# One masked conditional matrix kernel: where the first masks are loaded, and which engine masks and splits around units 5 to 7

## The chip, the core and the metric

One NeuronCore of a Trainium2 chip. The metric is the device time of one execution in microseconds, the median over several runs. Engines by name: TensorE (PE; weight loads are listed apart as PEld), VectorE (DVE), ScalarE (ACT), GpSimd (POOL) and SyncE (SP), which issues most DMAs.

## The reference

```
masked_w = weight * mask[None, :, :]            # weight (8, 256, 256), mask (256, 256)
w_bot    = einsum('bg,got->bot', y, masked_w)   # y (32, 8)
out      = x + einsum('bnt,bot->bno', x, w_bot) + bias   # x (32, 256, 256), fp32
```

For each of 32 batch entries a 256x256 matrix is mixed from 8 masked weight matrices; x is multiplied by it (and by the identity, for the residual), and a bias is added.

## The kernel before

**Making the matrices.** The 32 matrices live transposed in `w_raw` (t on partitions, o on columns). They are made in 8 units of 32 output rows (`UNITS`, `SPAN`), two units to a pair. The rows of a unit fall into a diagonal side, on which the identity must be added, and another ("off") side. The weights of the diagonal side are multiplied by the mask ahead of the matmuls ("masked" loads: 512 columns of weights and 512 of mask side by side, into a staging place in `x_ring`; the product goes into `blocks`), and PE starts these banks with a 0/1 matmul that writes the identity (L326). The weights of the other side go in unmasked ("other" loads), and the mask is applied when the PSUM result is copied into `w_raw`: by VectorE (L635) for all units but unit 1, where ScalarE copies (L516) and GpSimd masks in place (L315, four instructions, semaphore `raw_masked`). ScalarE copies the diagonal side of each unit (L534; VectorE L631 for unit 1). PE's small matmuls are `weigh` (L332).

Who masks the diagonal weights: VectorE pairs 0 and 3 (L581, two halves each, `masked_by_dve`), GpSimd pairs 1 and 2 (L306, `masked_by_pool`).

**The products.** x comes in 8 groups of 4 batch entries. Group 0 is multiplied in plain fp32 (L451): 8 matmuls ("early", between units 5 and 6; ScalarE evicts them at L531) and 24 more after unit 7. Groups 1 to 7 are multiplied as three matmuls of rounded numbers each: high weights by high x (L431), high weights by low x (L432), low weights by high x (L433). ScalarE casts the high parts (L491 x, L499 and L502 weights), VectorE subtracts the low ones (L589 x, L598 and L605 weights). Group 1's weights are split in three pieces (`pieces`): half of the batch entries of output half 0, the other half of them, and all of output half 1. Group 2 is split whole.

**Order.** Each engine's order is written out by hand. SP issues: other 0, masked 0, masked 1, other 1, off (masks of the off sides of units 2 to 7), masked 2, other 2, half of x group 0, masked 3, other 3, the other half, group 1; then, waiting for the masks of pairs 0 and 1, group 2, and for those of pairs 2 and 3, group 3. ScalarE's queue loads `smalls` (y, bias, the off masks of units 0 and 1) first. ScalarE around unit 6: copy of unit 5, pieces 0 and 1 (L502), early eviction (L531), copies of units 6 and 7, then, once all of `w_raw` is there, piece 2, high x of group 1 in two halves, high weights and x of group 2. VectorE there: units 4, 5 (L635), masks of pair 3 (L581), low pieces 0 and 1 (L605), units 6 and 7, then low piece 2, low x of group 1, and so on. PE's batch of 24 starts when seven copies of ScalarE are done (`raw_by_act`, `UNITS - 1`, L471), and its last 16 when all copies are (L474, L475). PE's unit 2 needs other 1 and, for its diagonal side, masks of pair 1 by GpSimd.

## Time and profile before

| | us |
|---|---|
| median of 3 runs | 66.35 (66.0 to 66.44) |
| span of the profiled execution | 65.5 |
| PE busy / DVE / ACT / POOL | 58.8 / 48.1 / 47.9 / 7.0 |
| PE's granted clock | 0.999 of 2.4 GHz |

The span runs from the first to the last instruction of one profiled execution; the median is of timed runs, which hold what lies around the span too. A row of a timeline gives start, duration, engine, line, operation, output and inputs, count, and in brackets the idle time before it and what ended it. Rows of like instructions that follow each other are merged, and their duration then runs from the first start to the last end.

### The profile page before, as it was taken

To read this page: it belongs to the slowest core of one execution; us is meant where nothing else is said; L and a number is where in the kernel's file an instruction comes from. 1 tells how busy PE (TensorE), PEld (TensorE's weight loads), DVE (VectorE), ACT (ScalarE), POOL (GpSimd) and SP (SyncE) were. 2 spreads that over 40 slices of the span, in tenths; PEclk is the share of its full clock that TensorE was granted. 3 is DMA by queue.
4 is the path that set the end of the run, shared out by engine and by line. 5 is a ranking of instruction groups with operands and counts; after the bars stand their busy time and mean duration, and the time that the engine had idled before them with its cause. 6 is when DMAs were issued, how large, how long until landed. Compare 5 with 4: busy or idle time off the path is not lost.

```text
span 65.5 us, 1501 instructions
## 1 busy us (share of the span) xinstructions
PE 58.8 (90%) x645; PEld 54.3 (83%) x645; DVE 48.1 (73%) x36; ACT 47.9 (73%) x40; POOL 7.0 (11%) x17
## 2 busy tenths in 40 slices
PE   2997188999999999999999999999999999999910
PEld 1266087977888899999999999999999999999900
DVE  2109809999957989999999999989999992250200
ACT  2506609799889999999999799999869986005520
POOL 5500299900000000000000000000000000000000
PEclk9999999999999999999999999999999999999999
DMA  0999999999998157954999999999999229918393
GB/s 0 260 373 306 352 412 422 407 434 428 420 410 340 60 85 255 408 215 198 245 285 225 400 451 420 403 441 423 398 413 425 93 100 408 398 63 325 158 372 116
DMA packets 5334, 20.21 MB, mean 309 GB/s; under 512 B 592, under 2 KB 1104, under 8 KB 4432
## 3 DMA queue, kind: packets, MB, share of 16 engines
q1 hardware_dynamic: 5040, 19.89, 79.6%
q10 hardware_dynamic: 288, 0.23, 1.1%
q8 instruction: 5, 0.08, 0.5%
q14 instruction: 1, 0.01, 0.1%
HBM read 11.73 MB, written 8.39 MB: 307 GB/s over the span
## 4 chain that ended last, share of the span: by engine, by line
PE 79%; DMA 9%; ACT 4%; SPq 2%; issue 1%
PE slots L433 20%; PE slots L431 20%; PE slots L432 20%; PE slots L451 11%; DMA weights<-in_first 9%; PE slots L332 6%; ACT w_raw L534 3%; PE slots L326 2%; ACT weights L563 1%; SPq L230 1%; SPq L222 1%; SPq L229 1%
## 5 line engine op out<-in xcount | busy, mean ns | idle before, releaser
L431 PE MATMUL slots<-x_hi,w_hi 128*128 128x256 f32 x112 | 31.4, 280 | 0.0
L432 PE MATMUL slots<-x_lo,w_hi 128*128 128x256 f32 x112 | 31.2, 279 | 0.0
L433 PE MATMUL slots<-x_hi,w_lo 128*128 128x256 f32 x112 | 31.2, 279 | 0.0
L431 PEld LDWEIGHTS slots<-x_hi,w_hi 128*128 128x128 f32 x112 | 21.1, 188 | 0.0
L432 PEld LDWEIGHTS slots<-x_lo,w_hi 128*128 128x128 f32 x112 | 21.1, 188 | 0.0
L433 PEld LDWEIGHTS slots<-x_hi,w_lo 128*128 128x128 f32 x112 | 21.1, 188 | 0.0
L589 DVE TENSOR_TENSOR x_lo<-x_ring,x_hi 128x2048 fp32r<-128x2048 f32 (+1 forms) x8 | 16.1, 2022 | 0.5 <-ACT x_hi L491 0.5
L491 ACT CAST x_hi<-x_ring 128x2048 fp32r<-128x2048 f32 (+1 forms) x8 | 13.5, 1694 | 1.3 <-DMA x_ring<-in_x 1.3
L511 ACT ACTIVATE weights<-slots,smalls 128x1024 f32<-128x1024 f32 x10 | 10.8, 1112 | 4.7 <-PE slots L433 4.7
L598 DVE TENSOR_TENSOR w_lo<-w_raw,w_hi 128x2048 fp32r<-128x2048 f32 x6 | 13.7, 2288 | 0.2 <-ACT w_hi L499 0.2
L499 ACT CAST w_hi<-w_raw 128x2048 fp32r<-128x2048 f32 x6 | 11.5, 1909 | 0.0
L332 PE MATMUL slots<-smalls,weights 32*128 32x128 f32 x256 | 9.3, 279 | 2.0 <-DMA weights<-in_first 1.6
L332 PEld LDWEIGHTS slots<-smalls,weights 32*128 32x128 f32 x256 | 8.2, 186 | 3.0 <-DVE w_raw L631 1.9
L534 ACT COPY w_raw<-slots 128x1024 f32<-128x1024 f32 x7 | 7.0, 1014 | 3.8 <-PE slots L332 3.7
L635 DVE TENSOR_TENSOR w_raw<-slots,masks_off 128x1024 f32<-128x1024 f32 x6 | 7.1, 1220 | 2.0 <-PE slots L332 1.8
L451 PE MATMUL slots<-x_ring,w_raw 128*128 128x256 f32 x32 | 7.4, 386 | 0.2
L451 PEld LDWEIGHTS slots<-x_ring,w_raw 128*128 128x128 f32 x32 | 5.9, 190 | 1.3 <-ACT w_raw L534 0.5
L615 DVE TENSOR_SCALAR weights<-slots,smalls 128x1024 f32<-128x1024 f32 x4 | 5.1, 1282 | 2.4 <-PE slots L433 2.4
L581 DVE TENSOR_TENSOR weights<-x_ring 128x256 f32<-128x256 f32 x4 | 1.5, 420 | 3.1 <-DMA x_ring<-in_first 3.1
L306 POOL TENSOR_TENSOR weights<-x_ring 128x256 f32<-128x256 f32 x4 | 2.8, 727 | 5.2 <-ACT w_raw L534 5.0
L440 PE MATMUL slots<-zeros 128*128 128x512 bf16 x5 | 2.3, 626 | 1.2 <-DVE zeros L571 1.2
L605 DVE TENSOR_TENSOR w_lo<-w_raw,w_hi 128x512 fp32r<-128x512 f32 (+1 forms) x3 | 2.5, 866 | 1.2 <-ACT w_hi L502 1.2
(25 smaller groups left out, 19.3 us busy)
## 6 DMA issues: line engine op xcount, KB each, us to landing
out<-weights SPq DMA_DIRECT2D x15, 512.0 KB, 4.7
x_ring<-in_x SPq DMA_DIRECT2D x7, 1024.0 KB, 9.6
x_ring<-in_first SPq DMA_DIRECT2D x6, 512.0 KB, 7.2
weights<-in_first SPq DMA_DIRECT2D x4, 256.0 KB, 6.6
out<-weights SPq DMA_DIRECT2D x1, 256.0 KB, 2.4
out<-weights SPq DMA_DIRECT2D x1, 128.0 KB, 2.3
out<-weights ACTq DMA_DIRECT2D x1, 128.0 KB, 2.1
smalls<-in_small ACTq DMA_DIRECT2D x1, 97.0 KB, 3.1
```

The source lines that it names most:

```text
L332: return nc.tensor.matmul(bank(u, i)[:, q * B * RT:(q + 1) * B * RT], weights_of(u, i // PER)[rows, q * P:(q + 1) * P], y[rows], start=not ...
L431: nc.tensor.matmul(dst, wh, xh, start=(k == 0), stop=False)
L432: nc.tensor.matmul(dst, wh, xl, start=False, stop=False)
L433: last = nc.tensor.matmul(dst, wl, xh, start=False, stop=(k == KC - 1))
L451: last = nc.tensor.matmul(dst[:, (b - lo) * N:(b - lo + 1) * N], w_raw[:, b, k * O + h * P:k * O + (h + 1) * P], x_ring[:, 0, first_x(k, b ...
L491: nc.scalar.copy(part_x(x_hi[:, g % RS], lo, hi), part_x(x_ring[:, g % XS], lo, hi)).then_inc(x_hi_ready, 1)
L499: nc.scalar.copy(part(w_hi, g), raw_part(g)).then_inc(w_hi_ready, 1)
L511: nc.scalar.activation(result(g, h), product(g, h), ACT.Identity, bias=bias(h)).then_inc(done, 1)
L534: nc.scalar.copy(raw_slot(u, True), made(u, True)).then_inc(raw_by_act, 1)
L589: nc.vector.tensor_tensor(part_x(x_lo[:, g % RS], lo, hi), part_x(x_ring[:, g % XS], lo, hi), part_x(x_hi[:, g % RS], lo, hi).bitcast(F32) ...
L598: nc.vector.tensor_tensor(part(w_lo, g), raw_part(g), part(w_hi, g).bitcast(F32), ALU.subtract).then_inc(w_lo_ready, 1)
L635: nc.vector.tensor_tensor(raw_slot(u, False), made(u, False), mask_off_of(u).unsqueeze(2).broadcast_to([P, PER * QU, B, RT]), ALU.mult).th ...
```

## The change

The masks of pair 0 depend on the output row and t, not on the group, so each stands 8 times in the 128 partitions. They are now loaded once, a quarter per partition (`mask_in`, 128 columns, at the end of `smalls`), and VectorE spreads them with four stream shuffles into the place where the loaded masks stood. VectorE masks half 0 of pair 0, GpSimd half 1 (`first_by_pool`). The off masks of units 0 and 1 leave `smalls` for a DMA of their own on ScalarE's queue (`first_offs`), and the bias goes to the end of the "off" load. GpSimd also masks pair 3, and makes pieces 0 and 1 of group 1's low weights (`w_lo_by_pool`). ScalarE casts output half 0 of group 2's weights ahead of the early eviction, the pieces 0 and 1 behind it, and piece 2 behind high x of group 1; VectorE subtracts that half of group 2 between units 5 and 6. PE gets one more matmul of zeros (512 columns) in unit 2. The two functions `lows_of` and `highs_of` give the semaphore counts that follow.

```diff
--- before.py
+++ after.py
@@ -43,21 +43,24 @@
 ORDER = (("other", 0), ("masked", 0), ("masked", 1), ("other", 1), ("off", 0), ("masked", 2), ("other", 2), ("x", 0),
          ("masked", 3), ("other", 3), ("x", 1))
-COLUMNS = {"masked": SLOT, "other": BANK, "off": (UNITS - SIDES) * SPAN, "x": WIDE // 2}
-AT_BIAS = B * RT
-AT_MASKS = AT_BIAS + HO
-SMALL = AT_MASKS + SIDES * SPAN
-def conditional_residual(nc, x, small, first, out):
+FIRST = {("masked", 0): BANK}
+COLUMNS = {"masked": SLOT, "other": BANK, "off": (UNITS - SIDES) * SPAN + HO, "x": WIDE // 2}
+CHUNKS = 4
+CHUNK = BANK // CHUNKS
+AT_SPREAD = B * RT
+SMALL = AT_SPREAD + CHUNK
+AT_BIAS = (UNITS - SIDES) * SPAN
+def conditional_residual(nc, x, small, first_off, first, out):
     assert QU * P == BANK and SLOT == 2 * BANK and O == N == T and QU * B * RT == BANK
-    assert SPAN * TILES == P and QU * RT * 2 == ROWS and KC == HO == SIDES == PER == 2 and TILES == QU == NB == SLOTS == PAIRS
+    assert SPAN * TILES == P and QU * RT * 2 == ROWS and KC == HO == SIDES == PER == 2 and TILES == QU == NB == SLOTS == PAIRS and CHUNKS <= G
     with ExitStack() as ctx:
         def sb(name, shape, dt=F32):
@@ -77,7 +80,8 @@
         weights = sb("weights", [P, SLOTS, SLOT])
-        masks_off = sb("masks_off", [P, UNITS - SIDES, PER * QU, RT])
+        offs = sb("offs", [P, COLUMNS["off"]])
+        first_offs = sb("first_offs", [P, SIDES, SPAN])
         smalls = sb("smalls", [P, SMALL])
         x_ring = sb("x_ring", [P, XS, WIDE])
         x_hi = sb("x_hi", [P, RS, WIDE], F32R)
@@ -104,22 +108,22 @@
             return blocks[:, 2 * (u // 2) + (side != diagonal_side(u)), :]
         def in_order(what, j):
-            at = P * sum(COLUMNS[kind] for kind, i in ORDER[:ORDER.index((what, j))])
-            return first[at:at + P * COLUMNS[what]].rearrange("(p f) -> p f", p=P)
+            at = P * sum(FIRST.get((kind, i), COLUMNS[kind]) for kind, i in ORDER[:ORDER.index((what, j))])
+            return first[at:at + P * FIRST.get((what, j), COLUMNS[what])].rearrange("(p f) -> p f", p=P)
         y = smalls[:, 0:B * RT]
         def mask_off_of(u):
             if u < SIDES:
-                return smalls[:, AT_MASKS + u * SPAN:AT_MASKS + (u + 1) * SPAN].rearrange("p (m r) -> p m r", r=RT)
-            return masks_off[:, u - SIDES]
+                return first_offs[:, u].rearrange("p (m r) -> p m r", r=RT)
+            return offs[:, (u - SIDES) * SPAN:(u - SIDES + 1) * SPAN].rearrange("p (m r) -> p m r", r=RT)
         def half_of(i):
             return slice(i * BANK // 2, (i + 1) * BANK // 2)
         def bias(h):
-            return smalls[:, AT_BIAS + h:AT_BIAS + h + 1]
+            return offs[:, AT_BIAS + h:AT_BIAS + h + 1]
         smalls_loaded = sem("smalls_loaded")
         zeroed = sem("zeroed")
@@ -129,7 +133,10 @@
         one_zeroed = sem("one_zeroed")
         one_ready = sem("one_ready")
-        masks_off_loaded = sem("masks_off_loaded")
+        mask_spread = sem("mask_spread")
+        first_by_pool = sem("first_by_pool")
+        first_offs_loaded = sem("first_offs_loaded")
+        offs_loaded = sem("offs_loaded")
         masked_loaded = [sem(f"masked_loaded{j}") for j in range(PAIRS)]
         others_loaded = [sem(f"others_loaded{j}") for j in range(PAIRS)]
         masked_by_dve = sem("masked_by_dve")
@@ -149,6 +156,7 @@
         x_lo_ready = sem("x_lo_ready")
         w_hi_ready = sem("w_hi_ready")
         w_lo_ready = sem("w_lo_ready")
+        w_lo_by_pool = sem("w_lo_by_pool")
         early_ready = sem("early_ready")
         early_by_act = sem("early_by_act")
         products_ready = sem("products_ready")
@@ -176,6 +184,14 @@
         pieces = ((0, NB // 2, 0), (NB // 2, NB, 0), (0, NB, 1))
+        def lows_of(g, h):
+            return g + 1 if g > 2 else (None, (None, 2), (1, 3))[g][h]
+        def highs_of(g, h):
+            return g + 3 if g > 2 else (None, (3, 4), (1, 5))[g][h]
         def raw_part(g, lo=0, hi=NB, h=None):
             v = w_raw[:, NB * g + lo:NB * g + hi, :]
             return v if h is None else v.rearrange("p b (k o) -> p b k o", k=KC)[:, :, :, h * P:(h + 1) * P]
@@ -227,9 +243,9 @@
                 return sp.dma_start(x_ring[:, 0, i * SLOT:(i + 1) * SLOT], in_order("x", i))
             sp.dma_start(blocks[:, 1, :], in_order("other", 0)).then_inc(others_loaded[0], 16)
-            sp.dma_start(staged(0), in_order("masked", 0)).then_inc(masked_loaded[0], 16)
+            sp.dma_start(staged(0)[:, 0:BANK], in_order("masked", 0)).then_inc(masked_loaded[0], 16)
             load_pair(1)
-            sp.dma_start(masks_off[:].rearrange("p u m r -> p (u m r)"), in_order("off", 0)).then_inc(masks_off_loaded, 16)
+            sp.dma_start(offs[:], in_order("off", 0)).then_inc(offs_loaded, 16)
             load_pair(2)
             load_half(0).then_inc(half_x_loaded, 16)
             load_pair(3)
@@ -237,12 +253,12 @@
             load_group(1)
-            sp.wait_ge(masked_by_dve, 2)
+            sp.wait_ge(masked_by_dve, 1)
+            sp.wait_ge(first_by_pool, 1)
             sp.wait_ge(masked_by_pool, 2)
             load_group(XS - 2)
-            sp.wait_ge(masked_by_pool, 2 * (PAIRS - 2))
-            sp.wait_ge(masked_by_dve, 4)
+            sp.wait_ge(masked_by_pool, 2 * (PAIRS - 1))
             load_group(XS - 1)
             for g in range(GROUPS - 1):
@@ -298,8 +314,13 @@
                 one_of[:], firsts[:, 0:QU * RT].rearrange("p (q r) -> p q r", r=RT).unsqueeze(2).broadcast_to([P, QU, B, RT]),
             ).then_inc(one_ready, 1)
-            behind_pair = (None, (0,), (1, 2, 3))
-            for j in range(1, PAIRS - 1):
+            pool.wait_ge(masked_loaded[0], 16)
+            pool.wait_ge(mask_spread, CHUNKS)
+            nc.gpsimd.tensor_tensor(blocks[:, 0, half_of(1)], staged(0)[:, 0:BANK][:, half_of(1)],
+                                    staged(0)[:, BANK:SLOT][:, half_of(1)], ALU.mult).then_inc(first_by_pool, 1)
+            behind_pair = (None, (0,), (1, 2, 3), ())
+            for j in range(1, PAIRS):
                 pool.wait_ge(masked_loaded[j], 16)
                 for i in range(2):
@@ -308,12 +329,18 @@
                 if j == 1:
-                    pool.wait_ge(smalls_loaded, 16)
+                    pool.wait_ge(first_offs_loaded, 16)
                     pool.wait_ge(raw_by_act, 1)
                 for i in behind_pair[j]:
                     some = raw_columns(1, False)[:, i * MB:(i + 1) * MB, :]
-                    nc.gpsimd.tensor_tensor(some, some, smalls[:, AT_MASKS + SPAN:AT_MASKS + 2 * SPAN].unsqueeze(1).broadcast_to(
+                    nc.gpsimd.tensor_tensor(some, some, first_offs[:, 1].unsqueeze(1).broadcast_to(
                         [P, MB, SPAN]), ALU.mult).then_inc(raw_masked, 1)
+            for i in range(HO):
+                pool.wait_ge(w_hi_ready, i + 2)
+                nc.gpsimd.tensor_tensor(part(w_lo, 1, *pieces[i]), raw_part(1, *pieces[i]), part(w_hi, 1, *pieces[i]).bitcast(F32),
+                                        ALU.subtract).then_inc(w_lo_by_pool, 1)
         @block.tensor
         def _(pe):
@@ -350,9 +377,12 @@
                         if q == QU - 1:
                             last.then_inc(others_ready, 1)
                 for q in range(QU):
-                    if q % 2 == 0:
-                        pe.wait_ge(masked_by_dve, q // 2 + 1)
+                    if q == 0:
+                        pe.wait_ge(masked_by_dve, 1)
+                    if q == QU // 2:
+                        pe.wait_ge(first_by_pool, 1)
                     for u in range(SIDES):
                         for i in range(PER):
                             last = weigh(u, on[u] + i, q)
@@ -374,6 +404,8 @@
                     pe.wait_ge(early_by_act, 1)
                 identity(u, on)
                 identity(u, on + 1)
+                if u == SIDES:
+                    nc.tensor.matmul(bank(u, on), zeros[:, 0:P], zeros[:], start=False, stop=False)
                 pe.wait_ge(raw_by_dve, u - 1)
                 if u % 2 == 0:
@@ -382,10 +414,7 @@
                 weigh(u, off, 0)
                 weigh(u, off + 1, 0)
                 for q in range(QU):
-                    if u == EARLY and q % 2 == 0:
-                        pe.wait_ge(masked_by_dve, 3 + q // 2)
-                    elif u % 2 == 0 and q % 2 == 0:
+                    if u % 2 == 0 and q % 2 == 0:
                         pe.wait_ge(masked_by_pool, u - 1 + q // 2)
                     weigh(u, on, q)
@@ -401,7 +430,10 @@
                 pe.wait_ge(x_lo_ready, 1 if g == 1 else g + 1)
-                pe.wait_ge(w_lo_ready, 1 if g == 1 else g + len(pieces) - 1)
+                if g == 1:
+                    pe.wait_ge(w_lo_by_pool, 1)
+                else:
+                    pe.wait_ge(w_lo_ready, lows_of(g, 0))
                 for h in range(HO):
                     if g >= 2 and h == 0:
@@ -417,10 +449,10 @@
                         if g == 1 and h == 0 and b == NB // 2:
                             pe.wait_ge(x_lo_ready, 2)
-                            pe.wait_ge(w_lo_ready, 2)
-                        if g == 1 and h == 1 and b == 0:
-                            pe.wait_ge(w_lo_ready, len(pieces))
+                            pe.wait_ge(w_lo_by_pool, 2)
+                        if g <= 2 and h == 1 and b == 0:
+                            pe.wait_ge(w_lo_ready, lows_of(g, 1))
                         if g == GROUPS - 1 and h == 1 and b == NB - 1:
                             pe.wait_ge(out0_by_act, g)
@@ -481,6 +513,7 @@
         @block.scalar
         def _(act):
             act.dma_start(smalls[:], small).then_inc(smalls_loaded, 16)
+            act.dma_start(first_offs[:].rearrange("p u f -> p (u f)"), first_off).then_inc(first_offs_loaded, 16)
             def high_x(g, lo=0, hi=NB):
@@ -490,13 +523,13 @@
                     act.wait_ge(products_ready, HO * (g - RS + 1))
                 nc.scalar.copy(part_x(x_hi[:, g % RS], lo, hi), part_x(x_ring[:, g % XS], lo, hi)).then_inc(x_hi_ready, 1)
-            def high_weights(g):
+            def high_weights(g, h=None):
                 act.wait_ge(raw_masked, NB * g // MB + 1)
                 if g > RS:
                     act.wait_ge(products_ready, HO * (g - RS + 1))
-                nc.scalar.copy(part(w_hi, g), raw_part(g)).then_inc(w_hi_ready, 1)
+                nc.scalar.copy(part(w_hi, g, 0, NB, h), raw_part(g, 0, NB, h)).then_inc(w_hi_ready, 1)
             def high_piece(i):
                 nc.scalar.copy(part(w_hi, 1, *pieces[i]), raw_part(1, *pieces[i])).then_inc(w_hi_ready, 1)
@@ -522,24 +555,24 @@
                     act.wait_ge(raw_by_act, UNITS // HO)
                     act.wait_ge(raw_by_dve, UNITS // HO)
-                    act.wait_ge(raw_masked, 1)
+                    high_weights(2, 0)
+                    act.wait_ge(offs_loaded, 16)
+                    act.wait_ge(early_ready, 1)
+                    nc.scalar.activation(result(0, 0)[:, 0:BANK], early, ACT.Identity, bias=bias(0)).then_inc(early_by_act, 1)
                     high_piece(0)
                     high_piece(1)
-                    act.wait_ge(smalls_loaded, 16)
-                    act.wait_ge(early_ready, 1)
-                    nc.scalar.activation(result(0, 0)[:, 0:BANK], early, ACT.Identity, bias=bias(0)).then_inc(early_by_act, 1)
                 act.wait_ge(diagonal_ready, u + 1)
                 nc.scalar.copy(raw_slot(u, True), made(u, True)).then_inc(raw_by_act, 1)
             act.wait_ge(raw_by_act, UNITS)
             act.wait_ge(raw_by_dve, UNITS)
-            high_piece(2)
             for lo in (0, NB // 2):
                 high_x(1, lo, lo + NB // 2)
-            high_weights(2)
+            high_piece(2)
             high_x(2)
+            high_weights(2, 1)
             act.wait_ge(products_ready, 1)
             nc.scalar.activation(result(0, 0)[:, BANK:SLOT], product(0, 0)[:, BANK:SLOT], ACT.Identity,
@@ -574,14 +607,19 @@
             nc.vector.tensor_reduce(firsts[:], ident[:].rearrange("p (i f) -> p f i", i=TILES), axis=AX_X,
                                     op=ALU.add).then_inc(firsts_ready, 1)
-            def mask_pair(j):
+            def mask_pair(j, halves):
                 dve.wait_ge(masked_loaded[j], 16)
-                for i in range(2):
+                for i in halves:
                     nc.vector.tensor_tensor(blocks[:, 2 * j, half_of(i)], staged(j)[:, 0:BANK][:, half_of(i)],
                                             staged(j)[:, BANK:SLOT][:, half_of(i)], ALU.mult).then_inc(masked_by_dve, 1)
-            mask_pair(0)
+            dve.wait_ge(smalls_loaded, 16)
+            for c in range(CHUNKS):
+                nc.vector.stream_shuffle(staged(0)[:, BANK + c * CHUNK:BANK + (c + 1) * CHUNK], smalls[:, AT_SPREAD:AT_SPREAD + CHUNK],
+                                         [G * (r // G) + c for r in range(ROWS)]).then_inc(mask_spread, 1)
+            dve.wait_ge(mask_spread, CHUNKS // 2)
+            mask_pair(0, (0,))
             def low_x(g, lo=0, hi=NB):
@@ -589,20 +627,13 @@
                 nc.vector.tensor_tensor(part_x(x_lo[:, g % RS], lo, hi), part_x(x_ring[:, g % XS], lo, hi),
                                         part_x(x_hi[:, g % RS], lo, hi).bitcast(F32), ALU.subtract).then_inc(x_lo_ready, 1)
-            def low_weights(g):
-                dve.wait_ge(w_hi_ready, g + len(pieces) - 1)
+            def low_weights(g, h=None):
+                dve.wait_ge(w_hi_ready, highs_of(g, h))
                 if g > LS:
                     dve.wait_ge(products_ready, HO * (g - LS + 1))
-                nc.vector.tensor_tensor(part(w_lo, g), raw_part(g), part(w_hi, g).bitcast(F32),
-                                        ALU.subtract).then_inc(w_lo_ready, 1)
-            def low_piece(i):
-                dve.wait_ge(w_hi_ready, i + 1)
-                nc.vector.tensor_tensor(part(w_lo, 1, *pieces[i]), raw_part(1, *pieces[i]), part(w_hi, 1, *pieces[i]).bitcast(F32),
+                nc.vector.tensor_tensor(part(w_lo, g, 0, NB, h), raw_part(g, 0, NB, h), part(w_hi, g, 0, NB, h).bitcast(F32),
                                         ALU.subtract).then_inc(w_lo_ready, 1)
             def finish(g):
@@ -615,15 +646,13 @@
                 nc.vector.tensor_scalar(result(g, 1), product(g, 1), bias(1), None,
                                         ALU.add).then_inc(out1_by_dve, 1)
-            dve.wait_ge(smalls_loaded, 16)
+            dve.wait_ge(first_offs_loaded, 16)
             for u in range(UNITS):
                 if u == SIDES:
-                    dve.wait_ge(masks_off_loaded, 16)
+                    dve.wait_ge(offs_loaded, 16)
                 if u == EARLY:
-                    mask_pair(PAIRS - 1)
-                    low_piece(0)
-                    low_piece(1)
+                    low_weights(2, 0)
                 if u == 1:
@@ -636,11 +665,11 @@
                                         mask_off_of(u).unsqueeze(2).broadcast_to([P, PER * QU, B, RT]),
                                         ALU.mult).then_inc(raw_by_dve, 1)
-            low_piece(2)
             for lo in (0, NB // 2):
                 low_x(1, lo, lo + NB // 2)
-            low_weights(2)
+            low_weights(1, 1)
             low_x(2)
+            low_weights(2, 1)
             finish(0)
             for g in range(1, GROUPS - 1):
                 if g + 2 < GROUPS:
...
+    mask_in = np.stack([diagonal[1][p, p % G % CHUNKS * CHUNK:(p % G % CHUNKS + 1) * CHUNK] for p in range(P)])
+    loads["masked", 0] = diagonal[0]
...
+    loads["off", 0] = np.concatenate([other_off, bias.reshape(HO, P).T], axis=1)
...
+    small = np.concatenate([y.reshape(P, B * RT), mask_in], axis=1)
```

## Rows read from the trace of the kernel before

**Rows 1.** The page: its head, and the chain's shares by engine and by line.
```profile
span 65.5 us, 1501 instructions
...
PE 79%; DMA 9%; ACT 4%; SPq 2%; issue 1%
PE slots L433 20%; PE slots L431 20%; PE slots L432 20%; PE slots L451 11%; DMA weights<-in_first 9%; PE slots L332 6%; ACT w_raw L534 3%; PE slots L326 2%; ACT weights L563 1%; SPq L230 1%; SPq L222 1%; SPq L229 1%
```

**Rows 2.** The chain that ended last, in order of time: start us, us, what.
```profile
2.11 6.18 DMA weights<-in_first
...
8.43 1.34 PE slots L332 x30
...
13.42 1.99 PE slots L451 x8
...
16.68 1.02 ACT w_raw L534
17.75 5.45 PE slots L451 x24
```

**Rows 3.** Busy us by stretches, 30 to 40: PE, PEld, DVE, ACT, POOL, clock, DMA.
```profile
30.00:40.00 10.00, 10.00 (x88) 10.00 (x87) 10.00 (x6) 9.63 (x7) 0.00 (x0) 1.00 0.94 324
```

**Rows 4.** Transfers: a stretch (GB/s last), the queues, two issues, two landings.
```profile
2.50:8.50 6.00, 4.00 (x77) 2.29 (x75) 3.03 (x4) 2.02 (x2) 0.95 (x3) 1.00 0.99 356
...
q1 hardware_dynamic: 5040, 19.89, 79.6%
q10 hardware_dynamic: 288, 0.23, 1.1%
...
0.75 0.40 ACTq L483 DMA_DIRECT2D smalls<-in_small  x1
...
5.09 0.66 SPq L222 DMA_DIRECT2D x_ring<-in_first  x1
...
smalls<-in_small ACTq DMA_DIRECT2D x1, 97.0 KB, 3.1
...
x_ring<-in_first SPq DMA_DIRECT2D x1, 512.0 KB, 9.1
```

**Rows 5.** Timeline of ACT, 14 to 22 us.
```profile
14.39 1.14 ACT L502 CAST w_hi<-w_raw 128x512 fp32r<-128x512 f32 x2
15.52 0.69 ACT L531 ACTIVATE weights<-slots,smalls 128x512 f32<-128x512 f32 x1
16.68 2.00 ACT L534 COPY w_raw<-slots 128x1024 f32<-128x1024 f32 x2 [0.48 <-PE slots L332]
19.01 1.05 ACT L502 CAST w_hi<-w_raw 128x1024 fp32r<-128x1024 f32 x1 [0.33 <-DVE w_raw L635]
19.96 2.00 ACT L491 CAST x_hi<-x_ring 128x1024 fp32r<-128x1024 f32 x2
```

**Rows 6.** Timeline of DVE, 1 to 34 us.
```profile
1.50 0.37 DVE L574 TENSOR_REDUCE firsts<-ident 128x32 f32<-128x128 f32 x1 [0.37 <-POOL ident L284]
4.99 0.76 DVE L581 TENSOR_TENSOR weights<-x_ring 128x256 f32<-128x256 f32 x2 [3.11 <-DMA x_ring<-in_first]
...
14.57 0.75 DVE L581 TENSOR_TENSOR weights<-x_ring 128x256 f32<-128x256 f32 x2
...
16.56 2.36 DVE L635 TENSOR_TENSOR w_raw<-slots,masks_off 128x1024 f32<-128x1024 f32 x2
20.09 1.23 DVE L605 TENSOR_TENSOR w_lo<-w_raw,w_hi 128x1024 fp32r<-128x1024 f32 x1 [1.17 <-ACT w_hi L502]
...
31.60 2.29 DVE L598 TENSOR_TENSOR w_lo<-w_raw,w_hi 128x2048 fp32r<-128x2048 f32 x1
```

**Rows 7.** Timeline of POOL, 7 to 14 us.
```profile
7.71 1.41 POOL L306 TENSOR_TENSOR weights<-x_ring 128x256 f32<-128x256 f32 x2 [5.05 <-ACT w_raw L534]
...
9.91 1.42 POOL L306 TENSOR_TENSOR weights<-x_ring 128x256 f32<-128x256 f32 x2 [0.20 <-DMA x_ring<-in_first]
11.29 1.84 POOL L315 TENSOR_TENSOR w_raw<-w_raw,smalls 128x256 f32<-128x256 f32 x3
```

10 lines of the change are left out of this document (5 added, 5 removed).

## The prediction

> **What bounds the kernel now.** I read first the page's head and its chain that ended last [rows 1]: 65.5 us of span, 79% of the chain on PE. Then the chain piece by piece, in order of time [rows 2]. It falls into two parts. From 17.75 us on it is PE alone: 24 matmuls of line 451 take 5.45 us, to 23.20, and group 1 follows without a pause. Groups 1 to 7 (L431, L432, L433, each 20% of the span on the chain, [rows 1]) are 39.3 us, 5.6 a group, to about 62.5; in the stretch from 30 to 40 us PE is busy 10.00 of 10.00 [rows 3]. The last eviction and store end the span. The diff leaves this part alone. So the time falls only if the batch that starts at 17.75 starts earlier.
>
> What sets 17.75? Read [rows 2] backwards: ACT's copy of unit 6 (L534, 16.68 to 17.70; L471 counts seven copies, that one among them), before it the early product (L451 x8, 13.42 to 15.41) and units 6 and 7, before that units 2 to 5, in which PE and ACT take turns, and before 8.43 a wait for pair 1's unmasked rows, which landed at 2.11 + 6.18 = 8.29. A transfer, then a chain of some 9.3 us.
>
> **How far the transfers move.** "masked 0" falls from 512 to 256 KB. The smalls grow from 97 KB (194 columns) to 128 KB (256 columns), and 32 KB (64 columns) become a DMA of their own, with 256 bytes per partition. In all 193 KB fewer lie ahead of masked 1 and other 1; "off" gains 8 bytes per partition, nothing. From 2.5 to 8.5 us the queues moved 356 GB/s [rows 4], at which 262 thousand bytes are 0.74 us; by queue q1's mean (79.6% of 16 engines x 65.5 us for 19.89 MB, so 42 ns per thousand bytes of one engine) they are 0.69. Against it stand 31 KB more of smalls, 0.09 us, and the new DMA: by its bytes 0.09 us, by its 128 packets at q10's mean (288 packets in 1.1% of 16 x 65.5 us, 40 ns each) 128 x 40 / 16 ns = 0.32 us. So the loads behind land earlier by S = 0.74 - 0.09 - 0.09 = 0.56 us by the kind prices and 0.69 - 0.09 - 0.32 = 0.28 by the dear ones. I take 0.45, a little above the middle, for this reason: GpSimd could start on masked 1 at 7.71 [rows 7], VectorE on masked 0 at 4.99 [rows 6]: 2.7 us for 512 KB, which are 1.5 us at 356 GB/s, so some of the 16 engines ran behind the mean. If removed bytes count at the pace of the laggards (1672 thousand bytes landed between about 2.0 and 8.3 us, 265 GB/s), S is 198 / 265 = 0.75. That is the upper end.
>
> All that follows 8.43 moves by S, for units 2 to 5 wait for one another and for loads that move alike (masked 2, for which GpSimd waited 0.20 us until 9.91, [rows 7]).
>
> **The first pair.** The smalls were issued at 0.75 and landed 3.1 later, at 3.85 [rows 4], and will at 3.95. VectorE then spreads them with four shuffles of 128 columns. No row has one. From below: VectorE's subtraction takes 1.23 us for 1024 columns and 2.29 for 2048, 1.04 ns a column, and the two 256-column masks 0.76 together, so some 0.36 each; 128 columns fewer make 0.23. From above: the reduction of 128 columns, 0.37 [rows 6]. Four of them are 0.9 to 1.5 us. I take 0.25 each, since a copy stands nearer to the mask than a reduction does, and the spread ends at 4.95. Half 0 is masked at 5.35 (at dearest 5.9) instead of 5.4. GpSimd's half takes 0.73 [rows 7] and is there at 5.7 to 6.2, or at 6.6 if it must wait for VectorE's; PE comes to it some 0.6 us after it starts. The pair's weighs (1.3 us for as many, [rows 2]) end at 6.6 to 7.3. The cover is the wait for other 1, now until 8.29 - 0.45 = 7.84: this costs nothing. Without that cover it would be up to 0.7 us. The zero matmul added at unit 2 (512 columns; it can't be dearer than the 0.6 that remain, being one instruction among matmuls of 0.28) lies in the same wait. ScalarE's second DMA issue (the first is 0.40 us, [rows 4]) comes before its table load, long before its first copy.
>
> The Trainium skill (VectorE: DVE Perf Modes, The perf-mode tier table) gives a stream shuffle about 2400 ns for 2048 elements whatever the type; an estimate by it, 0.15 us of streaming each and a fixed part, would lie near my lower bound. No row of before shows one.
>
> **The middle, units 5 to 7.** Here work moves between engines, and the sum turns on ScalarE [rows 5]. Before: from 14.39 the two pieces (1.14 together; start to start a row is 0.10 shorter, as 19.01 + 1.05 against 19.96 shows), at 15.52 the early eviction behind its product (15.41), then 0.48 us idle, and at 16.68 unit 6's copy. After, in the old times less S: the cast of the third group's first half (128x1024, as the row at 19.01, 0.95 start to start) takes the place at 14.39 and is through at 15.34; the early eviction still starts with its product, at 15.52; 0.59 later, at 16.11, the two pieces, 1.04; unit 6's copy at 17.15. PE's unit 6 is done by 16.65, so the copy now waits for ScalarE itself. 17.15 against 16.68: of 0.95 us added, 0.48 fill the idle time and **0.47 go onto the path**. PE's batch of 24 then starts at 17.75 + 0.47 - S = 17.77 with S = 0.45.
>
> VectorE [rows 6] loses the masks of pair 3 and pieces 0 and 1 (14.57 to 16.56) and gains half of the third group's low (128x1024, 1.23). It can start when the cast ends, 15.44 - 0.45 = 15.0, to 16.2; units 6 and 7 (2.36) follow to 18.6, before 18.92. PE needs unit 7's result (L475) 8 matmuls into the batch, at 17.8 + 1.8 = 19.6: no gain, no loss. GpSimd: masked 3 landed at 5.09 + 9.1 = 14.19 [rows 4] and now at 13.75; GpSimd is free by 13.13 - 0.45; the two halves (1.41, [rows 7]) end at 15.2. PE starts unit 6 at 14.9 and asks for the second half some 0.7 us later: hidden, with 0.4 to spare. Then it makes pieces 0 and 1 of the low matrices, 512 columns each. No row has that form on GpSimd; by its masks (0.69 per 256 columns, start to start) one is 1.4 us, and if the rounding form is twice as dear, 2.8. From 16.7 on they end at 19.5 or 22.3. Group 1 needs them at 23.2: nothing. SP's load of x for group 3 waits for the masks of pair 3, at 15.2 against 14.57 + 0.75 = 15.3: nothing.
>
> **What is late next.** If PE did start earlier, would it run into VectorE? The low matrices of group 3 are ready at 31.60 + 2.29 = 33.89 [rows 6], needed at 23.2 + 2 x 5.6 = 34.4: 0.5 us to spare. The change makes this 1.7, since a half of 1.2 us moves ahead of the batch. So no later wait eats a gain; but there is none to eat.
>
> **The sum**, against the profiled 65.5 us: -0.45 (transfers) + 0.47 (ScalarE) = 0.0. The runs shown have a median of 66.35, 0.85 above this span; the same distance is to be added after. I forecast 66.3, as S has more room above my value than below.
>
> **The rivals.**
> *A. Removed bytes count at the laggards' pace*: S = 0.75, gain 0.28, 66.05. For it speaks the 2.7 us between masked 0 and masked 1; against it that the mean rate of all engines doesn't show it.
> *B. The shift comes through whole*, ScalarE's cast being hidden: gain 0.45 to 0.75, 65.9 to 65.6. Against it: ScalarE's order is written out, and 0.48 us is all its idle time there.
> *C. The small packets and the shuffles eat the shift*: S at 0.28 or lower, to 0; or shuffles of 0.6 us each, by which the first pair ends near 8.0. Loss 0.2 to 0.47, 66.55 to 66.8.
> *D, the other side: VectorE and GpSimd shut each other out.* If VectorE's low half (15.0 to 16.2, both inputs in SBUF) starts before GpSimd's second half of pair 3 (due at 14.45), and the later has to wait for the earlier, GpSimd ends at 16.9, PE's unit 6 near 17.6, its copy at 18.65, and the batch starts at 18.7: 0.95 us late, 67.3. It decides from the point where masked 3 lands more than 0.55 us later than 13.75. GpSimd's two pairs of masks took 1.41 and 1.42 us, with VectorE idle for much of the first and at work for the second [rows 6, 7], but at work on matrices in PSUM, so the trace doesn't refute it. In the forecast's order the same would cost VectorE 0.2 us, of which it has 1.0.
> The Trainium skill (SBUF — State Buffer, Who interferes with whom) says that a VectorE instruction with two SBUF inputs and a GpSimd instruction that reads SBUF block one another for a whole instruction. By that rule the shutting out is real and only the order decides whether the time is 66.3 or 67.3.
>
> **How the numbers follow.** Forecast (66.15 to 66.5) 0.50; A 0.18; B 0.10; C 0.14; D 0.08. The range, 65.85 to 66.8, holds the forecast, A and C and leaves out D and most of B. A measurement of this kernel tells some 1%, 0.66 us, from no change. Faster by more: B with a large S, and a little beyond A, 0.12. Slower by more: D, and what lies beyond C, 0.12. Within it 0.76.
>
> **What would show it.** After: PE's first weigh of unit 2 at 7.9 to 8.1; no idle time on ScalarE before unit 6's copy, at about 16.7; line 451's batch at 17.7 to 17.8, group 1 right behind it at 23.2. The forecast is wrong if the batch starts before 17.4 (then ScalarE's cast was hidden, or S is large), or after 18.0 with PE waiting inside unit 6 (then D).

## The result, and the profile after

| | before | after |
|---|---|---|
| median, us | 66.33 (6 runs) | 67.15 (6 runs) |
| span, median of the timed runs' own spans | 64.6 (113 later runs, 64.2 to 65.9) | 64.95 (6 runs, 64.6 to 65.5) |
| time less span, median | 1.80 (1.74 to 1.90) | 2.19 (2.17 to 2.23) |
| span of the profiled execution | 65.5 | 64.9 |

The changed kernel is slower by 1.3%: ratio 1.013, 95% interval 1.0098 to 1.0162. I had forecast 66.3. Ratios, and from here on the medians of span and of time less span, leave out executions over 1.5% above the fastest of their kernel; times, and the spans of the kernel before in this table, leave out none. Yet its profile shows a shorter span than the one before, 64.9 against 65.5. Both are true, and the table says how. Every timed run also gives its span. The kernel before has spans from 64.2 to 65.9 in 113 runs with a median of 64.6 (64.5 by the rule for ratios), and 108 of them are shorter than the 65.5 of the profile that I read; and the time is 1.80 us more than the span, not the 0.85 that I got by taking the median of other runs less that one span. After, the time is 2.19 more than the span. So the loss of 0.8 us is 0.35 to 0.45 in the span and 0.4 outside it.

The page of the kernel after, its head and the chain's shares by engine (compare [rows 1]):

```profile
span 64.9 us, 1516 instructions
...
PE 77%; ACT 8%; DMA 6%; issue 2%; DVE 2%; ACTq 0%
```

Its chain in order of time (start us, us, what), against [rows 2]:

```profile
0.74 3.69 DMA smalls<-in_small
...
4.46 0.67 DVE x_ring L619 x5
...
5.27 0.42 DVE weights L614
...
5.74 1.31 PE slots L359 x32
7.05 0.20 PE slots L353 x2
7.26 0.32 PE slots L408
7.58 1.17 PE slots L359 x32
...
13.37 1.05 ACT w_hi L532
...
14.49 0.69 ACT weights L562
15.18 1.02 ACT w_hi L535 x2
16.20 0.92 ACT w_raw L567
...
17.17 5.45 PE slots L483 x24
```

Two things have changed. The transfer that stood on the chain (other 1) is gone from it: in its place stands the load of the smalls, then the shuffles, half 0's mask and the pair's weighs, then the new matmul of zeros, and unit 2 starts at 7.58. And from 13.37 to 17.12 the chain is ScalarE without a break: cast, early eviction, two pieces, copy of unit 6.

ScalarE's timeline of the same stretch, against [rows 5]:

```profile
13.37 1.05 ACT L532 CAST w_hi<-w_raw 128x1024 fp32r<-128x1024 f32 x1
14.49 0.69 ACT L562 ACTIVATE weights<-slots,offs 128x512 f32<-128x512 f32 x1
15.08 1.13 ACT L535 CAST w_hi<-w_raw 128x512 fp32r<-128x512 f32 x2
16.11 1.93 ACT L567 COPY w_raw<-slots 128x1024 f32<-128x1024 f32 x2
```

The 0.48 us of idle time before unit 6's copy is gone. From the first cast to that copy it is 16.11 - 13.37 = 2.74 us; before it was 16.68 - 14.39 = 2.29. That is 0.45 more.

### The profile page after: what moved, and what is told of

It reads as the page before. It is cut to its first block, busy times and chain, and to the rows that moved or that the text cites. A ratio compares the mean times of both kernels' runs of the same rounds, so it can differ in the third digit from the quotient of the medians.

```text
span 64.9 us, 1516 instructions
## 1 busy us (share of the span) xinstructions
PE 59.5 (92%) x646; PEld 54.4 (84%) x646; DVE 47.4 (73%) x40; ACT 47.9 (74%) x41; POOL 12.1 (19%) x22
## 4 chain that ended last, share of the span: by engine, by line
PE 77%; ACT 8%; DMA 6%; issue 2%; DVE 2%; ACTq 0%
PE slots L464 20%; PE slots L463 20%; PE slots L465 20%; PE slots L483 8%; PE slots L359 7%; DMA smalls<-in_small 6%; ACT w_raw L567 3%; ACT w_hi L532 2%; ACT w_hi L535 2%; PE slots L353 1%; ACT weights L562 1%; DVE x_ring L619 1%; ACT weights L596 1%; DVE weights L614 1%; PE slots L408 0%
## 5 line engine op out<-in xcount | busy, mean ns | idle before, releaser
L463 PE MATMUL slots<-x_hi,w_hi 128*128 128x256 f32 x112 | 31.4, 280 | 0.0
L463 PEld LDWEIGHTS slots<-x_hi,w_hi 128*128 128x128 f32 x112 | 21.1, 188 | 0.0
L636 DVE TENSOR_TENSOR w_lo<-w_raw,w_hi 128x2048 fp32r<-128x2048 f32 (+1 forms) x8 | 15.5, 1931 | 0.8 <-ACT w_hi L532 0.8
L544 ACT ACTIVATE weights<-slots,offs 128x1024 f32<-128x1024 f32 x10 | 10.8, 1111 | 5.1 <-PE slots L465 5.1
L532 ACT CAST w_hi<-w_raw 128x2048 fp32r<-128x2048 f32 (+1 forms) x7 | 11.6, 1662 | 0.0
L567 ACT COPY w_raw<-slots 128x1024 f32<-128x1024 f32 x7 | 7.0, 1015 | 1.7 <-PE slots L359 1.5
L664 DVE TENSOR_TENSOR w_raw<-slots,offs 128x1024 f32<-128x1024 f32 x6 | 7.1, 1216 | 0.5 <-PE slots L359 0.4
L646 DVE TENSOR_SCALAR weights<-slots,offs 128x1024 f32<-128x1024 f32 x4 | 5.1, 1280 | 2.4 <-PE slots L465 2.4
L327 POOL TENSOR_TENSOR weights<-x_ring 128x256 f32<-128x256 f32 x6 | 4.3, 730 | 1.7 <-DMA x_ring<-in_first 1.5
L684 DVE TENSOR_SCALAR weights<-slots,offs 128x256 f32<-128x256 f32 x1 | 0.5, 483 | 3.6 <-PE slots L465 3.6
L549 ACT COPY w_raw<-slots 128x1024 f32<-128x1024 f32 x1 | 1.0, 1012 | 2.8 <-PE slots L359 2.8
```

The lines of the kernel that those rows point to most:

```text
L463: nc.tensor.matmul(dst, wh, xh, start=(k == 0), stop=False)
L532: nc.scalar.copy(part(w_hi, g, 0, NB, h), raw_part(g, 0, NB, h)).then_inc(w_hi_ready, 1)
L544: nc.scalar.activation(result(g, h), product(g, h), ACT.Identity, bias=bias(h)).then_inc(done, 1)
L567: nc.scalar.copy(raw_slot(u, True), made(u, True)).then_inc(raw_by_act, 1)
L636: nc.vector.tensor_tensor(part(w_lo, g, 0, NB, h), raw_part(g, 0, NB, h), part(w_hi, g, 0, NB, h).bitcast(F32), ALU.subtract).then_inc(w_l ...
L664: nc.vector.tensor_tensor(raw_slot(u, False), made(u, False), mask_off_of(u).unsqueeze(2).broadcast_to([P, PER * QU, B, RT]), ALU.mult).th ...
```

## The experiments

All times are medians of runs timed beside runs of the kernel before on the same chip; "time less span" is taken run by run. Two questions: where the 0.4 us outside the span come from, and where the gain of the transfers went.

**1. A fourth input tensor?** The off masks moved behind the smalls in one DRAM tensor:

```diff
-            act.dma_start(smalls[:], small).then_inc(smalls_loaded, 16)
-            act.dma_start(first_offs[:]..., first_off).then_inc(first_offs_loaded, 16)
+            act.dma_start(smalls[:], small[0:P * SMALL].rearrange("(p f) -> p f", p=P)).then_inc(smalls_loaded, 16)
+            act.dma_start(first_offs[:]..., small[P * SMALL:].rearrange("(p f) -> p f", p=P)).then_inc(first_offs_loaded, 16)
```

> The changed kernel, with one difference: the off masks of units 0 and 1 lie behind the smalls in the same DRAM tensor, so the program has three input tensors as before and not four; the DMA itself stays. Theory I (a fourth input tensor costs some 1.4 us before or after the span): the time falls from 67.15 to about 65.7, the span stays at 64.9, and time less span goes back from 2.2 to about 0.85. Theory W (the 1.4 us come from new work: shuffles, four more semaphores, the extra DMA): the time stays at 67.1, time less span at 2.2.

Measured: 66.99 us, ratio 1.0115 (1.0084 to 1.0147), time less span 2.19. Theory I expected 65.7 and fell. The execution profiled was a long one of 69.22 us with a span of 67.0; the last section comes back to it.

**2. The small DMA alone in the kernel before.**

```diff
+            act.dma_start(first_offs[:].rearrange("p u f -> p (u f)"), first_off).then_inc(first_offs_loaded, 16)
-small = np.concatenate([y.reshape(P, B * RT), bias.reshape(HO, P).T, first_off], axis=1)
+small = np.concatenate([y.reshape(P, B * RT), bias.reshape(HO, P).T], axis=1)
```

> The kernel before, with the off masks of units 0 and 1 taken out of the smalls into an input tensor and a DMA of their own on ScalarE's queue, nothing else. Theory I: span 65.5 to 65.8 and time less span 2.2, so 67.7 to 68.0. Theory W with the shuffles or the semaphores at fault: time less span stays 0.85, the time 66.3 to 66.7. Theory W with the DMA at fault gives the same as theory I here; the next kernel tells them apart.

Measured: 66.29 us, ratio 0.9992 (0.9959 to 1.0026), time less span 1.77. The DMA and the tensor together cost nothing that can be measured.

**3. An unread tensor.**

```diff
-    for name, a in (("x", x_in), ("small", small), ("first", first_in)):
+    for name, a in (("x", x_in), ("small", small), ("unused", first_off), ("first", first_in)):
```

> The kernel before, with a fourth input tensor that no instruction reads. Theory I in the form that every tensor of the program costs: 67.7. Theory I in the form that only a tensor which an engine addresses costs (its address must be fetched by that engine): 66.35, no change. Theory W: 66.35.

Measured: 66.68 us, ratio 1.0022 (0.9984 to 1.006), time less span 1.80. An unread tensor costs nothing either. This run brought the first doubt about my baseline: its instructions are those of the kernel before, and its span was 64.9. Its chain:

```profile
2.11 5.14 DMA weights<-in_first
...
7.38 1.16 PE slots L332 x28
...
16.79 5.45 PE slots L451 x24
```

Other 1 lands at 7.25, where [rows 2] have 8.29, and all that follows is 1.0 us earlier.

**4. The shuffles as such?** In the kernel before, into a tile that nobody reads:

```diff
+            for c in range(4):
+                nc.vector.stream_shuffle(dead[:, c, :], ident[:], [G * (r // G) + c for r in range(ROWS)])
```

> The kernel before, with four stream shuffles of 128 columns added on VectorE right after the identity's reduction, into a tile that nobody reads, where VectorE waits for the first pair anyway. Theory S (having stream shuffles in the program is what adds 0.40 us outside the span): span as before, 64.6, time less span 2.19 instead of 1.79, time 66.8. Theory N (the 0.40 us come from the number of semaphores or from other new instructions): 66.4, time less span 1.79.

Measured: 67.09 us, ratio 1.0064 (1.0017 to 1.011), time less span 2.08 (1.81 to 2.12), span 64.6 as before. Most of theory S's 2.19 is there, and not theory N's 1.79, so for now the shuffles were suspected.

**5. The changed kernel without the spread** (masks of pair 0 loaded whole):

```diff
-FIRST = {("masked", 0): BANK}
+FIRST = {}
-            for c in range(CHUNKS):
-                nc.vector.stream_shuffle(...).then_inc(mask_spread, 1)
```

> The changed kernel, but the masks of pair 0 are loaded whole, as before, and not spread; all else as changed. Theory S: time less span 1.79. Theory N: 2.1 to 2.19. In the span: if the spread delays the first pair (its weighs ended at 7.05 in the changed kernel, 6.8 in an execution of the kernel before), unit 2 starts when other 1 lands, near 7.4, the batch of 24 at 17.1, the span 64.8 to 64.9; if removed bytes were worth what I reckoned, unit 2 starts at 7.9 and the span is 65.3. Time by theory S 66.6 to 67.1.

Measured: 67.13 us, ratio 1.0127 (1.0063 to 1.0191), time less span 1.77, span 65.35 in only 4 runs. The part outside is gone, so something in the spread brings it; the span is longer by about as much, so here nothing is gained in total. A span of 65.3 was what I had expected if the removed bytes were worth what I had reckoned, so this run by itself speaks for the transfers; 7 and 17 will not. The chain:

```profile
2.11 5.79 DMA weights<-in_first
...
8.04 1.34 PE slots L357 x30
...
17.80 5.45 PE slots L481 x24
```

This execution had other 1 at 7.90, and from unit 2's start to the batch it takes 9.76 us.

**6. The cast undone.** The third group's weights whole and late again, on ScalarE and VectorE:

```diff
-                    high_weights(2, 0)
+                    high_piece(0)
+                    high_piece(1)
...
                     nc.scalar.activation(result(0, 0)[:, 0:BANK], early, ...).then_inc(early_by_act, 1)
-                    high_piece(0)
-                    high_piece(1)
...
-            high_weights(2, 1)
+            high_weights(2)
```

> The changed kernel, but ScalarE casts and VectorE splits the third group's weights whole and where the kernel before does; spread, GpSimd's masks and its low pieces as changed. If the cast ahead of the early eviction costs 0.47 us on ScalarE's way to the copy of unit 6, as the prediction has it: batch at 16.7 instead of 17.17, span 64.45, time 66.65 with 2.19 outside the span. If that cast lies hidden: span 64.9, time 67.1.

Measured: 67.19 us, ratio 1.0105 (1.0066 to 1.0143), time less span 2.19; median span 64.8. The medians don't settle 0.15 us. The profile does; its ScalarE:

```profile
13.15 1.14 ACT L535 CAST w_hi<-w_raw 128x512 fp32r<-128x512 f32 x2
14.45 0.69 ACT L564 ACTIVATE weights<-slots,offs 128x512 f32<-128x512 f32 x1 [0.16 <-PE slots L483]
15.62 2.00 ACT L567 COPY w_raw<-slots 128x1024 f32<-128x1024 f32 x2 [0.48 <-PE slots L359]
```

The early eviction starts at 14.45, as good as in the changed kernel (14.49), and unit 6's copy at 15.62 instead of 16.11. The idle 0.48 us is back. The cast costs 0.49 - 0.04 = 0.45 us on this piece of the path.

**7. The loads' part alone**, in the kernel before:

```diff
-            sp.dma_start(staged(0), in_order("masked", 0)).then_inc(masked_loaded[0], 16)
+            sp.dma_start(staged(0)[:, 0:BANK], in_order("masked", 0)).then_inc(masked_loaded[0], 16)
+            for c in range(4):
+                nc.vector.stream_shuffle(staged(0)[:, BANK + c * P:BANK + (c + 1) * P], smalls[:, AT_SPREAD:AT_SPREAD + P], ...)
```

> The kernel before with the loads' part of the change alone: masks of pair 0 loaded once and spread by four shuffles, VectorE masks both halves; off masks of units 0 and 1 in a tensor and DMA of their own; ScalarE's and GpSimd's work as before. Theory S: time less span 2.19. In the span: smalls land 0.6 us later (4.4), the spread ends at 5.4, the pair's weighs at 7.05, unit 2 starts near 7.4 to 7.5 whatever the loads: span 64.5 to 64.7, time 66.7 to 66.9. If the fewer bytes counted: span 64.2.

Measured: 66.83 us, ratio 1.0025 (0.9969 to 1.0082), time less span 1.98, span 64.7. In the span it is not told from the kernel before: 64.5 to 64.7 was expected if the fewer bytes did not count, 64.2 if they did. Its chain:

```profile
2.11 5.80 DMA weights<-in_first
...
8.05 1.34 PE slots L336 x30
...
17.37 5.45 PE slots L455 x24
```

193 KB fewer were ahead of other 1, and it landed at 7.91.

**8. Spread and cast both undone.** The edits of 5 and 6 together.

> The changed kernel with two parts undone: masks of pair 0 loaded whole and not spread, and the third group's weights cast and split whole and late. What is left of the change is the small DMA and GpSimd's new work. Both costs found so far gone: time less span 1.79, span as before 64.5 to 64.7, time 66.3 to 66.5, the kernel before's. If GpSimd's new work or the small DMA costs something by itself: 66.7 or more.

Measured: 66.64 us, ratio 1.0054 (1.002 to 1.0088), time less span 1.84, span 64.8. Of 1.3% there is 0.5% left. Whether that is GpSimd's new work, the zero matmul, or how six executions fell, isn't settled. In the one profiled, other 1 had landed at 7.3 and PE began unit 2 only at 7.86: its chain goes through the first pair's weighs, ScalarE's copy (6.15 to 7.17), the identity matmuls and the zero matmul behind them.

**9. The kernel before once more.**

> The kernel before once more, for a profile of another execution. If its shown profile (span 65.5, unit 2 started at 8.43) was one of the late landings: span 64.3 to 64.7, unit 2 at 7.2 to 7.5, batch of 24 near 16.7, time less span 1.8. If the shown profile was typical: 65.5 again, and time less span 0.85.

Measured: three runs of 66.8 to 66.93, spans 65.0 to 65.1, time less span 1.80; beside it 22 runs of the same kernel had a median of 66.39. The chain of this execution:

```profile
2.11 5.43 DMA weights<-in_first
7.68 1.34 PE slots L332 x30
...
16.98 5.45 PE slots L451 x24
```

The 1.8 us was as expected, the early landing was not: in the execution profiled it lay in between, and the three spans agree within 0.1 us. One launch of the kernel differs from the next by several tenths of a microsecond, in one and the same program.

**10, 11. One shuffle, sixteen shuffles**, of 16 columns each, dead, as in 4:

> The kernel before with one shuffle of 16 columns into a tile that nobody reads. If the time outside the span is a fixed price of having a shuffle in the program: time less span 2.1 to 2.2. If it grows with their number (0.1 each for four): 1.9.

> The same with sixteen shuffles of 16 columns. Fixed price: 2.1 to 2.2 again. Growing with their number: 3.4.

Measured: time less span 1.83 and 1.80, ratios 1.002 (0.9982 to 1.0058) and 1.0009 (0.9967 to 1.0052). Neither a fixed price nor one by number. Theory S fell.

**12 to 15. Length, number or kind.** Four shuffles of 128 columns again, four of 16, four copies, one shuffle of 128:

```diff
+                nc.vector.stream_shuffle(dead[:, c, 0:16], ident[:, 0:16], [G * (r // G) + c for r in range(ROWS)])
```
```diff
+                nc.vector.tensor_copy(dead[:, c, :], ident[:])
```

> Four dead shuffles of 128 columns in the kernel before, once more, as the measure for the next three on the same chip. If the first reading (time less span 2.07, 1.77 to 2.12) belonged to the kernel: 2.0 to 2.1 again. If it belonged to that chip or that hour: 1.8, like the shuffles of 16 columns.

> Four dead shuffles of 16 columns, same tile. If the length of the shuffles matters: 1.8. If something else in the four-column-block tile matters: as the kernel beside it.

> Four copies of 128 columns instead of the shuffles, same tile and place. If shuffling is what costs: time less span 1.8. If any new VectorE work or the tile costs: 2.05.

> One dead shuffle of 128 columns. If the price goes with the columns shuffled, a quarter of the excess: 1.87. If one long shuffle is enough: 2.05.

Measured, time less span: 2.08, 2.09, 2.22 and 1.79. Four plain copies cost more than four shuffles: it isn't the shuffling, and not the columns. Counting the instructions of VectorE's program as built, each shuffle as two (the timeline shows a LOAD_MASK_SELECT before each), the readings fall on one curve:

| VectorE's instructions | kernel | time less span, us |
|---|---|---|
| 48, 49 | 8; 5 | 1.84; 1.77 |
| 53 | before, 2, 3 | 1.80, 1.77, 1.80 |
| 55 | 10, 15 | 1.83, 1.79 |
| 57 | 14; 6 | 2.22; 2.19 |
| 58 | after, 1 | 2.19, 2.19 |
| 61 | 4, 12, 13 | 2.08, 2.08, 2.09 |
| 62 | 7 | 1.98 |
| 85 | 11 | 1.80 |

**16 to 18. The curve put to the test.** Sixteen dead copies of 16 columns in the kernel before, in the changed one, and in that of 6:

```diff
+            for c in range(16):
+                nc.vector.tensor_copy(dead[:, c, :], ident[:, 0:16])
```

> The kernel before with sixteen dead copies of 16 columns on VectorE, in its idle time behind the identity's reduction. Theory P (the time outside the span is set by where VectorE's program ends, by its number of instructions counting each shuffle twice: 1.8 up to 55, 2.2 at 57 and 58, 2.07 at 61, 1.98 at 62, 1.8 at 85): with 69 it is 1.8, time 66.4. Theory K (copies, or new work of VectorE, cost it, and the sixteen shuffles were an exception): 2.2 or more, time 66.8.

> The changed kernel with the same sixteen dead copies. Theory P: with 74 instead of 58, time less span falls from 2.19 to 1.8, the span stays at 64.9, the time is 66.7. Theory K: 2.2 or more, 67.1 or more.

> The changed kernel with the third group's weights cast late, as in an earlier run, and the sixteen dead copies. Theory P with the 0.47 us of the cast: time less span 1.8, span 64.5, the time 66.3, level with the kernel before. If the spread costs something of its own in the span: 66.6.

Measured, time less span: 1.82, 1.77 and 1.82, as theory P had said of all three. Work added to the changed kernel took 0.4 us off what lies outside its span. Times: the kernel before with the copies 66.28, ratio 1.0011 (0.9959 to 1.0062); the changed one 67.45, ratio 1.0114 (1.0025 to 1.0203), with spans of 64.8 and three times 65.6 to 65.8, so its time did not fall to the 66.7 that I expected; in the execution profiled, whose span was 65.6, other 1 landed at 7.58; the others have no profile. The third 66.72, ratio 1.0027 (0.9986 to 1.0069). With the cast undone, the program lengthened past the costly counts and the spread left in, the kernel can't be told from the one before. The chain of 17:

```profile
2.10 5.48 DMA weights<-in_first
...
7.71 1.36 PE slots L360 x30
...
17.50 5.45 PE slots L484 x24
```

No version beat the kernel before. The nearest, 2, 15 and 16, are level with it.

## Why the prediction was wrong

Two steps failed, and the forecast of 66.3 was short by both: the 0.45 us taken off for the transfers did not come, for the wait that they were to shorten was 0.4 us (run 3) or 0.6 (run 9) in other executions and not 1.6, and the first pair's new path now held unit 2 until 7.58; and "the same distance is to be added after" put the part outside the span at no change, where it grew by 0.39 us. 66.3 + 0.45 + 0.39 is 67.14, measured 67.15. The third term, 0.47 us for the cast, held.

**The middle, units 5 to 7: right, to a few hundredths.** I had 0.47 us for the cast on ScalarE. The way from unit 2's first weigh to the batch doesn't contain the loads before it. In executions in which PE waited for other 1 it took, with the cast late, 17.75 - 8.43 = 9.32 us in [rows 2], 9.30 in 9 and 9.32 in 7; with the cast early 9.76 in 5 and 9.79 in 17. So 0.44 to 0.49 us, and 0.45 by ScalarE's own rows in 6. It was an addition to the path in exactly the place named. This way is not quite the same when unit 2 starts early: 9.41 us in 3 and 9.51 in 6, in which GpSimd, done with its earlier work, waited 0.83 us for masked 2 until 9.06. There an early unit 2 ran into the next load.

**How far the transfers move: the term of 0.45 us did not come.** The step took "all that follows 8.43 moves by S". That rested on one execution in which other 1 landed at 8.29. In others of the same loads it landed at 7.54 (9) and 7.25 (3), and over eleven of them from 7.09 to 8.29 with a median of 7.54; with 193 KB fewer at 7.1 (the changed kernel), 8.1 (1), 6.93 (6), 7.91 (7), 7.58 (17) and 7.2 (18). One and the same program landed at 7.54 and 8.29, and with a tensor that nobody reads at 7.25: a spread of 1.0 us, more than the 0.28 to 0.75 that I argued about. The laggards that I noted were a trait of that execution, not of the kernel: where landing is early, PE waits for other 1 from 6.98 or so (its two identity matmuls done) to 7.38 in run 3, 0.4 us, and 0.6 in 9. S couldn't be worth more than this wait. Whether 193 KB move the landing at all isn't shown. By the spans, the loads' part is worth nothing with the cast late (64.85 in 18, 64.8 in 8; 64.7 in 7 against 64.5 before), and 0.4 us with the cast early in the changed kernel (64.95 against 65.35 in 5), but 17 has the same loads as the changed kernel and 65.7.

**The first pair: wrong.** "The cover is the wait for other 1, now until 7.84: this costs nothing." With other 1 at 2.10 + 5.0 = 7.1 after the change, there was no cover left. The smalls landed at 4.43, not 3.95 (3.69 us after issue, 3.70 in run 1; 3.3 to 3.4 in runs 6, 7, 17 and 18, 3.1 to 3.3 where they are 64 to 97 KB), the pair's weighs ended at 7.05 and the zero matmul took 0.32 us more of the chain, which I had laid in an idle stretch. Unit 2 began at 7.58 against 7.38 in run 3; behind other 1 alone (0.14 us after its landing, as in [rows 2]) it would have begun at 7.24, so the first pair and the zero matmul cost 0.34 us here. The shuffles themselves were no dearer than reckoned: 0.30 long and 0.21 from start to start, just under my lower bound of 0.23, so the spread took 0.81 us (4.46 to 5.27) and not 1.0.

```profile
4.46 0.30 DVE L619 STREAM_SHUFFLE x_ring<-smalls 128x128 f32<-128x128 f32 x1
...
4.66 0.29 DVE L619 STREAM_SHUFFLE x_ring<-smalls 128x128 f32<-128x128 f32 x1
```

**The sum: two errors in the baseline.** I made the sum against 65.5 us and carried "0.85 above this span, the same distance to be added after". The first was an execution longer than 108 of the 113 spans later seen, the second a difference between different executions. In the sum the two cancel, for 65.5 + 0.85 is the median of the timed runs; what did not cancel was the 1.6 us of wait for other 1 that this execution showed. It spoiled my sign of being wrong too: "if the batch starts before 17.4 (then ScalarE's cast was hidden, or S is large)". The batch started at 17.17, the cast was not hidden, and no large S was shown; the 17.75 belonged to a late execution. Redone with what the runs gave: 64.5 + 0.45 (cast) + 0 (loads) + 2.19 = 67.1, measured 67.15. This sum is made after the fact and agrees better than the runs allow: with the cast late again, 6, 8 and 18 still have median spans of 64.8 to 64.85. By the medians the cast gave back only 0.15 us, and 0.3 us of the loss in the span have no cause shown.

**Nothing outside the span: a term that I didn't have.** 0.39 us, which goes with VectorE's program growing from 53 to 58 instructions. It is half the loss, and no row of the changed kernel's profile carries it. That what is added to VectorE's program moves it is shown by 4, 12 to 14 and 17; the last section has what the traces show of the reason.

**Rivals.** A and B, a larger S, are not borne out. C comes nearest by its sign, with loss from the shuffles' path and the smalls, but its price there was at most 0.47. D's 67.3 is nearest to the measured 67.15 by chance: it has its mechanism and not its order, and it cost the path nothing. In the changed kernel VectorE's half of the third group, with both inputs in SBUF, meets GpSimd's masks of pair 3 (timelines of POOL and DVE):

```profile
13.54 1.42 POOL L327 TENSOR_TENSOR weights<-x_ring 128x256 f32<-128x256 f32 x2 [1.34 <-DMA x_ring<-in_first]
```

```profile
14.45 1.59 DVE L636 TENSOR_TENSOR w_lo<-w_raw,w_hi 128x1024 fp32r<-128x1024 f32 x1 [0.82 <-ACT w_hi L532]
```

1.59 us for what takes 1.23 alone (the same instruction in 5 and 17, with GpSimd idle): as if it could begin only at 14.81, 0.15 before GpSimd's second half ended at 14.96. In run 5, where both mask pair 0 and VectorE starts first, at 5.19 against 5.23, it is GpSimd that takes longer, 0.97 us instead of 0.73 [rows 7]:

```profile
5.19 0.42 DVE L612 TENSOR_TENSOR weights<-x_ring 128x256 f32<-128x256 f32 x1 [3.31 <-DMA x_ring<-in_first]
5.23 0.97 POOL L317 TENSOR_TENSOR weights<-x_ring 128x256 f32<-128x256 f32 x1 [2.58 <-DMA x_ring<-in_first]
```

The later one waits, in both directions. The Trainium skill (SBUF — State Buffer, Who interferes with whom) says that a VectorE instruction with two SBUF inputs and a GpSimd instruction that reads SBUF contend, and that the order of issue decides which one blocks. These rows agree, with 0.36 and 0.24 us, both some 0.15 us less than the time that the other still had to run by its row. In the order that came it was hidden, as forecast for that order (0.2 us reckoned, 0.36 measured).

**Smaller steps that held:** GpSimd's two low pieces took 2.64 us for the 2.8 reckoned; group 1 followed the batch without a pause (L463 at 22.62, on the chain right behind 17.17 + 5.45); VectorE's relief was not needed.

## What to carry to other kernels

Before a sum is made against a profile, set that profile among the spans of the timed runs: a wait that ends a chain there may be the tail of its distribution, and the gain from shortening it is at most what the typical run waits. Work that is moved ahead on an engine's queue costs its duration less the idle time that it fills before the next waited-for instruction; that was right here to 0.03 us. When a change of a few tenths is to be judged, take time less span run by run as well: here it moved by 0.4 us, and no row inside the span shows it.
